# Softmax attention on one Trainium2 core: 64-row products for the maxima, sums in four blocks, the inverse spread by transfers

## The chip, the core and the metric

The kernel runs on one core of a Trainium2 chip. The metric is the device time of one execution in microseconds (us). It computes a small network of six stages on an input of 8 sequences of 512 tokens with 128 features; the change touches one of them, the softmax attention, which is about 40% of the time.

## The reference, cut to what matters

```python
def _L0_attn_ref(x, Wq, Wk, Wv, Wo, bo):          # x: 8 x 512 x 128, 16 heads of 64
    q = split_heads(x @ Wq.T); k = split_heads(x @ Wk.T); v = split_heads(x @ Wv.T)
    sim = jnp.einsum('bhid,bhjd->bhij', q, k) * scale
    attn = safe_softmax(sim)                       # e = exp(s - max); e / (sum(e) + 1e-10)
    out = jnp.einsum('bhij,bhjd->bhid', attn, v)
    return out.transpose(0, 2, 1, 3).reshape(B, N, INNER) @ Wo.T + bo

x = x + 0.5 * _L0_ffn_ref(_layernorm(x, axis=-1), ...)
x = x + _L0_attn_ref(_layernorm(x, axis=-1), ...)  # the stage of this change
x = x + 0.5 * _L0_ffn_ref(...)                     # then a mixture of experts, linear attention,
...                                                # and the experts again
```

## The kernel before, in words

The stages run one after the other; each is a block in which every engine follows its own written-out list, with semaphores between them. The attention stage (`attn_stage`, from L544) works on 64 pairs of heads (8 sequences, 8 pairs each). The loop variable g counts pairs, and one turn of it is called a period here. In period g the engines work on several pairs at once: TensorE projects queries, keys and values of pair g+2, makes the scores of pair g+1 for their maxima, makes the transposed scores of pair g for the exponentials, multiplies pair g-1 with its values, and puts pair g-2 through the output weights. Names, with i as the unit (head i//4, tile of 128 i%4):

- **project** (L840 to L860): three fp16 products of a high and a low part for q and k (512 columns each), twelve of 128 columns for v, all into the one bank `proj`. `high` (L751, ScalarE) writes the fp16 high part from that bank, `low` (L682, VectorE) the low part, `values_in` (L757) the values.
- **to_rows** (L598 to L612, the SyncE queue) copies the parts into operand buffers: `both` holds a head's q with high rows in partitions 0 to 63 and low rows in 64 to 127, and beside it q high once more with a row for the maximum; `kh` holds k high in both halves, `kl` k low and a row of constants. It is 10 transfers a pair.
- **scores** (L806): one fp16 product of 128 rows and 512 columns for each of 8 units, from `both` and `kh`, so q high and q low enter. **neg_max** (L663, VectorE) reduces it to 128 maxima. **max_turned** (L817) transposes the maxima of a head, once per head, `max_row` on VectorE (L671) scales them, and `max_row` on SyncE (L614) copies them into `both`: two small transfers a pair.
- **scores_turned** (L824, products at L836 and L837): two fp16 products of 512 columns per unit, with the maximum already subtracted. **exp** (L765, ScalarE) writes the exponentials `pT`. Two banks take turns, so a unit waits for the exponential two units before.
- GpSimd adds the four tiles of `pT` of each head (L648 to L656). **values** (L862) multiplies this by ones into `sums`, two products of 64 output rows and 512 columns (L868), so that all 128 rows of `sums` hold the sum that belongs to them; then eight products of 64 output rows (L875) into `pv`. `total_out` (L773) copies the sums, `inv_total` (L689) inverts 128x512 on VectorE, `normalise` (L693) multiplies.
- **output** (L879): four fp32 products.

A shared numbering of uses (`bank_use`, `score_use`, `turn_use`) makes the two `score` banks serve the eight scores and the two transposes in order. The order of TensorE in a period stands in its last loop:

```python
for i in range(UPP):                       # 8 units
    if live(g + 1): scores(g + 1, i)
    if live(g):     scores_turned(g, i)
    if i == 1 and live(g):     max_turned(g, 1)
    if i == 2 and live(g + 2): project(g + 2, 0)
    if i == 3: ...                         # output(g-2), project(g+2, 1), max_turned(g+1, 0), values(g-1)
    if i == 6 and live(g + 2): project(g + 2, 2)
```

The functions in full:

Of the kernel before, what the change touches and what calls it, by code (L numbers as in the profile page):

```python
# [10 lines left out]
F16 = mybir.dt.float16  # L11
# [532 lines left out]
def attn_stage(nc, mem, tag):  # L544

    with ExitStack() as ctx:
# [3 lines left out]
        M_UNIT = 64.0  # L552
        both = [s.sb(f"both{i}", [P, 2, 2, SEQ], F16) for i in range(RING)]
        kh = [s.sb(f"kh{i}", [P, 2, SEQ], F16) for i in range(RING)]
        kl = [s.sb(f"kl{i}", [P, 2, SEQ], F16) for i in range(RING)]
        part = [s.sb(f"part_{n}", [P, 2, SEQ], F16) for n in "qk"]
        vv = [s.sb(f"v{i}", [P, TPB, P]) for i in range(4)]
        pT = [s.sb(f"pT{i}", [P, 2, TPB, SEQ]) for i in range(2)]
        psum = [mem["w_attn"][:, i, :].rearrange("p (h q) -> p h q", h=2) for i in range(2)]
        total, rinv = mem["w_attn"][:, 2, 0:SEQ], mem["w_attn"][:, 2, SEQ:2 * SEQ]  # L560
        nmax = [s.sb(f"nmax{i}", [P, P]) for i in range(2)]
        mrow = [s.sb(f"mrow{i}", [TPB, P], F16) for i in range(2)]
        oT = [s.sb(f"oT{i}", [P, SEQ]) for i in range(2)]
        ones = mem["spare"][:, 0:DH]
# [3 lines left out]
        (set_up, proj_done, hi_done, lo_done, v_out, s_done, s_read, t_done, exp_done, chain, added, sums_done, total_done,  # L568
         rinv_done, pv_done, o_done, out_done, biased, x_added) = (s.sem(n) for n in (
             "set_up", "proj_done", "hi_done", "lo_done", "v_out", "s_done", "s_read", "t_done", "exp_done", "chain",  # L570
             "added", "sums_done", "total_done", "rinv_done", "pv_done", "o_done", "out_done", "biased", "x_added"))
        s_in = [s.sem(f"s_in{i}") for i in range(RING)]
        t_in = [s.sem(f"t_in{i}") for i in range(RING)]
        m_in = [s.sem(f"m_in{i}") for i in range(2)]
        S_DMAS, T_DMAS = 8, 2
# [3 lines left out]

        def bank_use(g, j):  # L580

            if g < 0:
                return j if j < 2 else j - 1
            if g == PAIRS_ALL - 1:
                return 9 + 10 * g
            return 9 + 10 * g + j

        UNIT_USE = (0, 1, 3, 4, 6, 7, 8, 9)
        TURN_USE = (5, 2)
        score_use = lambda g, i: bank_use(g - 1, UNIT_USE[i])  # L590
        turn_use = lambda g, head: bank_use(g - 1 + head, TURN_USE[head])

        with nc.Block() as block:

            @block.sync
            def _(sp):
                clear_spent(sp, mem)
                def to_rows(g, which, part_i):  # L598

                    src = part[which]  # L600
                    k = g % RING
                    for head in range(2):
                        rows = src[halves[head], part_i, :]
                        if which == 0 and part_i == 0:
                            sp.dma_start(both[k][0:DH, :, head, :], rows.unsqueeze(1).to_broadcast([DH, 2, SEQ])).then_inc(s_in[k], 16)
                        elif which == 0:
                            sp.dma_start(both[k][DH:P, 0, head, :], rows).then_inc(s_in[k], 16)
                        elif part_i == 0:
                            sp.dma_start(kh[k][0:DH, head, :], rows).then_inc(s_in[k], 16)
                            sp.dma_start(kh[k][DH:P, head, :], rows).then_inc(s_in[k], 16)  # L610
                        else:
                            sp.dma_start(kl[k][0:DH, head, :], rows).then_inc(t_in[k], 16)  # L612

                def max_row(g, head):  # L614

                    sp.wait_ge(s_read, turn_use(g, head) + 1)
                    sp.dma_start(both[g % RING][DH:DH + 1, 1, head, :].rearrange("o (t q) -> o t q", q=P), mrow[head][:])\
                      .then_inc(m_in[head], 16)

                sp.wait_ge(set_up, RING + 3)  # L620
# [42 lines left out]
            def _(dve):  # L663
                def neg_max(g, i):

                    head, qt = divmod(i, TPB)
                    use = score_use(g, i)
                    dve.wait_ge(s_done, use + 1)
                    nc.vector.tensor_reduce(nmax[head][:, qt:qt + 1], score[use % 2][:], AX.X, ALU.max, negate=True)\  # L669
                      .then_inc(s_read, 1)  # L670

                def max_row(g, head):

                    use = turn_use(g, head)
                    dve.wait_ge(s_done, use + 1)
                    if g:
                        dve.wait_ge(m_in[head], 16 * g)
                    nc.vector.tensor_scalar(mrow[head][:], score[use % 2][0:TPB, 0:P], 1.0 / M_UNIT, None, ALU.mult)\
                      .then_inc(s_read, 1)

                def low(g, which):

                    dve.wait_ge(hi_done, 2 * g + 1 + which)
                    scale = (DH ** -0.5 / W_ATTN, 1.0 / W_ATTN)[which]
                    pair = part[which]
                    nc.vector.scalar_tensor_tensor(out=pair[:, 1, :], in0=proj[:], scalar=scale, in1=pair[:, 0, :], op0=ALU.mult,
                                                   op1=ALU.subtract).then_inc(lo_done, 1)
# [12 lines left out]

                def add_x(b):

# [5 lines left out]
                nc.vector.memset(nmax[0][:], 0.0)  # L708
                nc.vector.memset(nmax[1][:], 0.0).then_inc(set_up, 1)
# [4 lines left out]
                dve.wait_ge(set_up, RING + 2)  # L714
# [963 lines left out]
```

## Time and profile before

| | |
|---|---|
| median of 3 runs | 2228.96 us (2228.8 to 2236.12) |
| the profiled execution, its own time | 2225.31 us |
| its span in the trace | 2223.6 us |
| TensorE busy in the span | 1599.6 us, 72% |
| VectorE busy | 1569.2 us, 71% |
| granted TensorE clock, mean | 0.882 |

Busy time is the union of the instructions of an engine. A TensorE record ends later than its columns have streamed, so records overlap, and the distance between two starts is what a product takes of the engine. SPq is the queue from which SyncE issues transfers; such an issue holds only the queue, and its data land later.

### The profile page before, as it was taken

Reading aid. Unit: us, or ns where it says so; the run is one execution under the profiler, and the core shown is the slowest. Engines: PE = TensorE matmul, PEld = TensorE weight load, DVE = VectorE, ACT = ScalarE, POOL = GpSimd, SP = SyncE. Lnnn points to the kernel's source line nnn. Section 1 sums busy time; section 2 is a strip of 40 time slices with the busy share of each in tenths; the row PEclk is TensorE's granted clock in tenths of the full one; section 3 lists DMA queues with packets and bytes.
Section 4 is the critical chain, followed back from the end, with each engine's and each line's share of the span. In section 5 each row is a group of like instructions: output and inputs, shape, how many; then the busy total and the mean of one; then the engine's idle time right before and its main releaser. Section 6 shows DMA issues by size and latency. Waiting matters only on the chain. (4 is left out here: it accounts for less than half of the span.)

```text
span 2223.6 us, 29789 instructions
## 1 busy us (share of the span) xinstructions
PE 1599.6 (72%) x9139; PEld 934.4 (42%) x9139; DVE 1569.2 (71%) x3212; ACT 912.8 (41%) x2102; POOL 1028.3 (46%) x1332
## 2 busy tenths in 40 slices
PE   0546389999999999999965563158658888830686
PEld 0334134444444444444423343135437767730453
DVE  5887778878788888877878886336467777752563
ACT  0112255555555555555522221035336676610452
POOL 0111245555555555555532224635435555546353
PEclk9889599999999999999987895579879999955898
DMA  6000022222222222222200000122300000001224
GB/s 186 0 0 1 23 63 58 58 58 58 63 59 61 60 59 58 58 58 59 62 9 1 0 0 24 56 77 80 104 16 1 1 1 1 1 32 62 75 81 145
DMA packets 126010, 104.05 MB, mean 47 GB/s; under 512 B 19680, under 2 KB 120480, under 8 KB 125856
## 3 DMA queue, kind: packets, MB, share of 16 engines
q1 hardware_dynamic: 111616, 77.75, 13.6%
q0 software_dynamic: 8704, 18.89, 2.5%
q10 hardware_dynamic: 5536, 5.52, 0.8%
q8 instruction: 77, 1.26, 0.2%
q14 instruction: 77, 0.63, 0.1%
HBM read 29.32 MB, written 22.30 MB: 23 GB/s over the span
## 5 line engine op out<-in xcount | busy, mean ns | idle before, releaser
L770 ACT ACTIVATE at_pT<-at_turned 128x512 f32<-128x512 f32 x512 | 305.6, 597 | 290.3 <-PE at_turned L837 271.2
L669 DVE TENSOR_REDUCE at_nmax<-at_score 128x1 f32<-128x512 f32 x512 | 337.1, 680 | 69.8 <-PE at_score L814 66.8
L648 POOL TENSOR_TENSOR m_rows<-at_pT 128x512 f32<-128x512 f32 x128 | 162.5, 1269 | 375.1 <-ACT at_pT L770 375.1
L691 DVE RECIPROCAL m_rows<-m_rows 128x512 f32<-128x512 f32 x64 | 214.6, 3353 | 37.7 <-ACT m_rows L776 37.7
L875 PE MATMUL at_pv<-at_pT,at_v 128*64 128x512 f32 x1024 | 230.6, 592 | 0.0
L814 PE MATMUL at_score<-at_kh,at_both 128*128 128x512 f16 x512 | 196.7, 385 | 22.6 <-DVE at_nmax L669 17.0
L1056 POOL DMA_INDIRECT by_token<-m_ysb,m_dest x144 | 138.2, 960 | 144.7 <-DVE m_ysb L1136 109.5
L836 PE MATMUL at_turned<-at_both,at_kh 128*128 128x512 f16 x512 | 194.9, 381 | 0.4 <-ACT at_pT L770 0.3
L837 PE MATMUL at_turned<-at_both,at_kl 128*128 128x512 f16 x512 | 194.8, 380 | 0.0
L656 POOL TENSOR_TENSOR m_rows<-m_rows,at_pT 128x512 f32<-128x512 f32 x128 | 162.8, 1272 | 10.6 <-ACT at_pT L770 0.7
L652 POOL TENSOR_TENSOR m_rows<-m_rows,at_pT 128x512 f32<-128x512 f32 x128 | 162.7, 1271 | 10.4 <-ACT at_pT L770 0.5
L1050 POOL DMA_INDIRECT by_expert<-m_rows,m_slot x128 | 123.7, 966 | 90.7 <-DVE m_slot L1099 53.0
L419 PE MATMUL f_gate<-m_wguT,f_xqT 128*128 128x352 f32 x128 | 63.1, 581 | 104.2 <-DVEq L337 102.9
L1307 PE MATMUL m_h<-m_w,m_x 128*128 x432 | 113.8, 400 | 33.1 <-DVE m_x L1113 23.2
L875 PEld LDWEIGHTS at_pv<-at_pT,at_v 128*64 128x64 f32 x1024 | 73.6, 137 | 146.2 <-issue 146.2
L365 POOL TENSOR_TENSOR f_hq<-f_hg,f_hsc 128x704 f32<-128x704 f32 x32 | 44.4, 1386 | 194.3 <-DVEq L341 194.3
L854 PE MATMUL at_proj<-m_rows 128*128 128x512 f16 x384 | 107.1, 389 | 18.6 <-DVE at_kl L716 10.3
L115 DVE TENSOR_SCALAR la_xn<-la_y,la_ln_mean,la_ln_rstd 128x128 f32<-128x128 f32 x192 | 81.6, 486 | 52.4 <-POOLq L1478 52.4
L381 ACT ACTIVATE f_silu<-f_gate 128x704 f32<-128x704 f32 x32 | 24.2, 757 | 219.7 <-PE f_up L420 219.7
L814 PEld LDWEIGHTS at_score<-at_kh,at_both 128*128 128x128 f16 x512 | 49.5, 97 | 145.5 <-DVE at_nmax L669 61.7
L1296 PE MATMUL m_x<-m_ident,m_xin 128*128 128x128 f32 x144 | 23.0, 284 | 88.6 <-DMA m_xin<-by_expert 88.6
L1124 DVE SCALAR_TENSOR_TENSOR m_g<-m_h,m_xin,m_silu 128x256 f32<-128x256 f32 x144 | 65.3, 478 | 28.1 <-ACT m_silu L1220 14.3
(309 smaller groups left out, 3685.0 us busy)
## 6 DMA issues: line engine op xcount, KB each, us to landing
at_both<-at_part_q SPq DMA_DIRECT2D x128, 128.0 KB, 2.4
at_kh<-at_part_k SPq DMA_DIRECT2D x256, 64.0 KB, 2.0
m_xin<-by_expert SPq DMA_DIRECT2D x144, 72.0 KB
at_both<-at_part_q SPq DMA_DIRECT2D x128, 64.0 KB, 2.1
at_kl<-at_part_k SPq DMA_DIRECT2D x128, 64.0 KB
m_rows<-by_token SPq DMA_DIRECT2D x32, 256.0 KB, 4.8
by_token<-m_ysb,m_dest POOLq DMA_INDIRECT x144
m_x<-in_x SPq DMA_DIRECT2D x8, 256.0 KB, 4.7
```

What stands on the lines that cost most here:

```text
L648: nc.gpsimd.tensor_tensor(acc, pT[g % 2][:, head, 0, :], pT[g % 2][:, head, 1, :], ALU.add).then_inc(chain, 1)
L652: nc.gpsimd.tensor_tensor(acc, acc, pT[g % 2][:, head, 2, :], ALU.add).then_inc(chain, 1)
L656: nc.gpsimd.tensor_tensor(acc, acc, pT[g % 2][:, head, 3, :], ALU.add).then_inc(added, 1)
L669: nc.vector.tensor_reduce(nmax[head][:, qt:qt + 1], score[use % 2][:], AX.X, ALU.max, negate=True)\
L691: nc.vector.reciprocal(rinv, total).then_inc(rinv_done, 1)
L770: nc.scalar.activation(pT[g % 2][:, head, kt, :], turned[i % 2][:], ACT.Exp).then_inc(exp_done, 1)
L814: nc.tensor.matmul(score[use % 2][:], both[k][:, 0, head, qt * P:(qt + 1) * P], kh[k][:, head, :], start=True, stop=True).then_inc(s_done, 1)
L836: nc.tensor.matmul(turned[i % 2][:], kh[k][:, head, tile], both[k][:, 0, head, :], start=True, stop=False)
L837: nc.tensor.matmul(turned[i % 2][:], kl[k][:, head, tile], both[k][:, 1, head, :], start=False, stop=True)\
L875: last = nc.tensor.matmul(pv[halves[head], :], vv[g % 4][:, kt, halves[head]], pT[g % 2][:, head, kt, :], start=(kt == 0), stop=(kt == TPB ...
L1050: nc.gpsimd.indirect_dma_start(dram_rows, bass.IndirectOffsetOnAxis(slot[:, k, t:t + 1], 0), rows[k][:, t, :], None).then_inc(scattered, 16)
L1056: nc.gpsimd.indirect_dma_start(mem["dram_y_all"], bass.IndirectOffsetOnAxis(dest[j // TPB % DESTS][:, j % TPB:j % TPB + 1], 0), ysb[q % YS ...
```

## The change

Six parts, all in `attn_stage`.

1. The scores for the maxima use the high parts alone, straight from the projected tiles in SBUF: 64 rows per head, the two heads in rows 0 to 63 and 64 to 127, one after the other in program order, into the two `score` banks. The high parts get two buffers each. The scores no longer wait for transfers.
2. One transpose of a 128x8 tile of maxima per pair, into a corner of the `sums` bank, one scaling and one transfer in place of two of each. It now comes behind the k rows of the next pair on SyncE.
3. The sums are four products of 32 output rows and 256 columns, each (head, half of the queries) in a block of 32 partitions. `total_out` and the reciprocal work on 128x256.
4. One row of each block is spread to the 64 partitions of its head by four transfers (`spread`), and `normalise` waits for these and runs one period later.
5. The values of pair g are projected in period g, at its end; `v` has two buffers, and `oT` one.
6. The order of every engine's list changes. SyncE in period g: q rows and k rows of g+2, `max_row(g+1)`, `spread(g-1)`. TensorE: eight units, the products with the values at the end of the period, with the transpose and the projection of v in between.

`high` now waits also for the scores of pair g-2 of its buffer, and `values_in(g)` for `values(g-2)`; the small helpers keep their forms (the diff is cut, its indentation shortened).

```diff
+def q_rows(g):
     k = g % RING
+    sp.wait_ge(hi_done, 2 * g + 1)
     for head in range(2):
+        sp.dma_start(both[k][0:DH, :, head, :],
+                     head_of[0][g % 2][halves[head], :].unsqueeze(1).to_broadcast([DH, 2, SEQ])).then_inc(q_in[k], 16)
+    sp.wait_ge(lo_done, 2 * g + 1)
+    for head in range(2):
+        sp.dma_start(both[k][DH:P, 0, head, :], rest_of[0][halves[head], :]).then_inc(q_in[k], 16)
+def k_rows(g):
+    k = g % RING
+    sp.wait_ge(hi_done, 2 * g + 2)
+    for head in range(2):
+        for half in halves:
+            sp.dma_start(kh[k][half, head, :], head_of[1][g % 2][halves[head], :]).then_inc(k_in[k], 16)
+    sp.wait_ge(lo_done, 2 * g + 2)
+    for head in range(2):
+        sp.dma_start(kl[k][0:DH, head, :], rest_of[1][halves[head], :]).then_inc(k_in[k], 16)
+def max_row(g):
+    sp.wait_ge(m_out, g + 1)
+    sp.dma_start(both[g % RING][DH:DH + 1, 1, :, :].rearrange("o h (t q) -> o (h t) q", q=P), mrow[:]).then_inc(m_in, 16)
+def spread(g):
+    sp.wait_ge(packed_done, g + 1)
+    if g:
+        sp.wait_ge(o_done, g)
+    for head in range(2):
+        for half in range(2):
+            first = (2 * head + half) * QUAD
+            sp.dma_start(rinv[halves[head], half * HALF:(half + 1) * HALF],
+                         packed[first:first + 1, :].unsqueeze(1).to_broadcast([1, DH, HALF])).then_inc(rinv_in, 16)
...
+sp.wait_ge(set_up, RING + 2)
 for g in PERIODS:
-    if live(g):
-        max_row(g, 1)
     if live(g + 2):
         if g + 2 >= RING:
             sp.wait_ge(t_done, 8 * (g + 3 - RING))
-        sp.wait_ge(hi_done, 2 * (g + 2) + 1)
-        to_rows(g + 2, 0, 0)
-        sp.wait_ge(lo_done, 2 * (g + 2) + 1)
-        to_rows(g + 2, 0, 1)
+        q_rows(g + 2)
+        k_rows(g + 2)
     if live(g + 1):
-        max_row(g + 1, 0)
-    if live(g + 2):
-        sp.wait_ge(hi_done, 2 * (g + 2) + 2)
-        to_rows(g + 2, 1, 0)
-        sp.wait_ge(lo_done, 2 * (g + 2) + 2)
-        to_rows(g + 2, 1, 1)
+        max_row(g + 1)
+    if live(g - 1):
+        spread(g - 1)
...
+def neg_max(g, qt):
+    if qt == 0 and g:
+        dve.wait_ge(m_done, g)
+    for head in range(2):
+        dve.wait_ge(s_done, 8 * g + 2 * qt + head + 1)
+        nc.vector.tensor_reduce(nmax[:, head * TPB + qt:head * TPB + qt + 1], score[head][:], AX.X, ALU.max, negate=True)\
+          .then_inc(s_read, 1)
...
-def inv_total(g):
+def invert(g):
     dve.wait_ge(total_done, g + 1)
-    nc.vector.reciprocal(rinv, total).then_inc(rinv_done, 1)
+    if g:
+        dve.wait_ge(rinv_in, 16 * R_DMAS * g)
+    nc.vector.reciprocal(packed, total).then_inc(packed_done, 1)
 def normalise(g):
     dve.wait_ge(pv_done, g + 1)
-    dve.wait_ge(rinv_done, g + 1)
-    if g >= 2:
-        dve.wait_ge(out_done, g - 1)
-    nc.vector.tensor_tensor(oT[g % 2][:], pv[:], rinv, ALU.mult).then_inc(o_done, 1)
+    dve.wait_ge(rinv_in, 16 * R_DMAS * (g + 1))
+    if g:
+        dve.wait_ge(out_done, g)
+    nc.vector.tensor_tensor(oT[:], pv[:], rinv, ALU.mult).then_inc(o_done, 1)
...
 for g in PERIODS:
     if live(g + 1):
         neg_max(g + 1, 0)
+    if live(g - 2):
+        normalise(g - 2)
+    if live(g + 1):
         neg_max(g + 1, 1)
-    if live(g):
-        max_row(g, 1)
+    if live(g + 2):
+        low(g + 2, 0)
     if live(g + 1):
         neg_max(g + 1, 2)
         neg_max(g + 1, 3)
     if live(g + 2):
-        low(g + 2, 0)
+        low(g + 2, 1)
     if live(g + 1):
-        max_row(g + 1, 0)
-    if live(g + 2):
-        low(g + 2, 1)
+        max_row(g + 1)
     if live(g - 1):
-        inv_total(g - 1)
-    if live(g + 1):
-        neg_max(g + 1, 4)
-        neg_max(g + 1, 5)
-    if live(g - 1):
-        normalise(g - 1)
-    if live(g + 1):
-        neg_max(g + 1, 6)
-        neg_max(g + 1, 7)
+        invert(g - 1)
...
 for g in PERIODS:
     if live(g):
         exp(g, 0)
         exp(g, 1)
-        exp(g, 2)
     if live(g + 2):
         high(g + 2, 0)
     if live(g):
-        exp(g, 3)
+        for i in range(2, 6):
+            exp(g, i)
     if live(g + 2):
         high(g + 2, 1)
+    if live(g):
+        exp(g, 6)
+        exp(g, 7)
     if live(g - 1):
         total_out(g - 1)
     if live(g):
-        for i in range(4, 7):
-            exp(g, i)
-    if live(g + 2):
-        values_in(g + 2)
-    if live(g):
-        exp(g, 7)
+        values_in(g)
...
+def scores(g, qt):
+    if qt == 0:
+        pe.wait_ge(hi_done, 2 * g + 2)
+    if g or qt:
+        pe.wait_ge(s_read, 8 * g + 2 * qt)
+    for head in range(2):
+        rows = halves[head]
+        nc.tensor.matmul(score[head][:], head_of[0][g % 2][rows, qt * P:(qt + 1) * P], head_of[1][g % 2][rows, :],
+                         start=True, stop=True).then_inc(s_done, 1)
+
+def max_turned(g):
+    pe.wait_ge(s_read, 8 * (g + 1))
+    if g:
+        pe.wait_ge(m_out, g)
+    if g >= 2:
+        pe.wait_ge(total_done, g - 1)
+    nc.tensor.transpose(max_bank, nmax[:], mem["ident"][:]).then_inc(m_done, 1)
...
-        pe.wait_ge(t_in[k], 16 * T_DMAS * (g // RING + 1))
-    if kt == 0:
-        pe.wait_ge(m_in[head], 16 * (g + 1))
+        pe.wait_ge(q_in[k], 16 * Q_DMAS * (g // RING + 1))
+        pe.wait_ge(k_in[k], 16 * K_DMAS * (g // RING + 1))
+        pe.wait_ge(m_in, 16 * (g + 1))
...
+    if which == 0:
+        if g >= 3:
+            pe.wait_ge(v_out, g - 2)
+        if g:
+            pe.wait_ge(lo_done, 2 * g)
     elif which == 1:
         pe.wait_ge(lo_done, 2 * g + 1)
-    elif which == 2:
-        pe.wait_ge(lo_done, 2 * g + 2)
+    else:
+        pe.wait_ge(lo_done, 2 * min(g + 3, PAIRS_ALL))
+        if g:
+            pe.wait_ge(v_out, g)
...
+def add_up(g):
     pe.wait_ge(added, 2 * (g + 1))
     if g:
         pe.wait_ge(total_done, g)
+    pe.wait_ge(m_out, min(g + 2, PAIRS_ALL))
     for head in range(2):
+        for half in range(2):
+            first = (2 * head + half) * QUAD
+            last = nc.tensor.matmul(sums[first:first + QUAD, 0:HALF], ones[:],
+                                    psum[g % 2][:, head, half * HALF:(half + 1) * HALF], start=True, stop=True)
     last.then_inc(sums_done, 1)
...
 for g in PERIODS:
     for i in range(UPP):
-        if live(g + 1):
-            scores(g + 1, i)
         if live(g):
             scores_turned(g, i)
-        if i == 1 and live(g):
-            max_turned(g, 1)
-        if i == 2 and live(g + 2):
+        if i % 2 == 0 and live(g + 1):
+            scores(g + 1, i // 2)
+        if i == 1 and live(g + 2):
             project(g + 2, 0)
-        if i == 3:
-            if live(g - 2):
-                output(g - 2)
-            if live(g + 2):
-                project(g + 2, 1)
-            if live(g + 1):
-                max_turned(g + 1, 0)
-            if live(g - 1):
-                values(g - 1)
-        if i == 6 and live(g + 2):
-            project(g + 2, 2)
+        if i == 3 and live(g - 2):
+            output(g - 2)
+        if i == 5 and live(g + 2):
+            project(g + 2, 1)
+    if live(g - 1):
+        add_up(g - 1)
+        values(g - 1, 0)
+    if live(g + 1):
+        max_turned(g + 1)
+    if live(g - 1):
+        values(g - 1, 1)
+    if live(g):
+        project(g, 2)
+    if live(g - 1):
+        values(g - 1, 2)
+        values(g - 1, 3)
```

## Rows read from the trace of the kernel before

**Rows 1.** The page: busy time by engine, and two lines of its 40 slices.

```profile
PE 1599.6 (72%) x9139; PEld 934.4 (42%) x9139; DVE 1569.2 (71%) x3212; ACT 912.8 (41%) x2102; POOL 1028.3 (46%) x1332
...
PE   0546389999999999999965563158658888830686
...
PEclk9889599999999999999987895579879999955898
```

**Rows 2.** Busy by window: start and end, length, engines, clock, DMA share, GB/s.

```profile
601.13:614.59 13.46, 13.15 (x74) 5.87 (x73) 10.81 (x15) 7.17 (x12) 7.58 (x6) 1.00 0.22 55
```

**Rows 3.** Timeline (start, length, engine, line, operation): reciprocals of consecutive periods.

```profile
611.90 3.35 DVE L691 RECIPROCAL m_rows<-m_rows 128x512 f32<-128x512 f32 x1 [0.44 <-ACT m_rows L776]
...
625.36 3.35 DVE L691 RECIPROCAL m_rows<-m_rows 128x512 f32<-128x512 f32 x1 [0.44 <-ACT m_rows L776]
...
639.31 3.35 DVE L691 RECIPROCAL m_rows<-m_rows 128x512 f32<-128x512 f32 x1 [0.44 <-ACT m_rows L776]
```

**Rows 4.** Timeline of one period, the lines on which durations and handovers rest.

```profile
608.17 1.05 PE L887 MATMUL at_out<-m_woT,at_oT 128*128 128x128 f32 x8
...
609.28 0.82 PE L854 MATMUL at_proj<-m_rows 128*128 128x512 f16 x3
...
609.94 0.27 PE L822 MATMUL at_score<-m_ident,at_nmax 128*128 128x128 f32 x1
...
610.14 1.08 PE L868 MATMUL at_sums<-m_rows 128*64 128x512 f32 x4
...
611.05 3.60 PE L875 MATMUL at_pv<-at_pT,at_v 128*64 128x512 f32 x16
...
614.59 0.39 PE L814 MATMUL at_score<-at_kh,at_both 128*128 128x512 f16 x1
...
614.82 0.38 PE L836 MATMUL at_turned<-at_both,at_kh 128*128 128x512 f16 x1
...
615.03 0.38 PE L837 MATMUL at_turned<-at_both,at_kl 128*128 128x512 f16 x1
...
615.17 1.22 DVE L669 TENSOR_REDUCE at_nmax<-at_score 128x1 f32<-128x512 f32 x2
...
615.45 1.89 ACT L770 ACTIVATE at_pT<-at_turned 128x512 f32<-128x512 f32 x3 [3.58 <-PE at_turned L837]
...
616.54 0.83 PE L858 MATMUL at_proj<-m_rows 128*128 128x128 f16 x12
```

**Rows 5.** Instruction groups from 500 to 900 us (busy, mean ns, idle before).

```profile
L669 DVE TENSOR_REDUCE at_nmax<-at_score 128x1 f32<-128x512 f32 x235 | 154.7, 680 | 28.1 <-PE at_score L814 26.7
...
L691 DVE RECIPROCAL m_rows<-m_rows 128x512 f32<-128x512 f32 x30 | 100.6, 3353 | 13.1 <-ACT m_rows L776 13.1
...
L814 PE MATMUL at_score<-at_kh,at_both 128*128 128x512 f16 x235 | 89.7, 382 | 7.0 <-DVE at_nmax L669 7.0
...
L686 DVE SCALAR_TENSOR_TENSOR at_part_k<-at_proj,at_part_k 128x512 f16<-128x512 f32 x30 | 20.8, 692 | 7.2 <-ACT at_part_k L755 7.2
...
L678 DVE TENSOR_SCALAR at_mrow<-at_score 4x128 f16<-4x128 f32 x59 | 16.2, 274 | 30.8 <-PE at_score L822 30.8
```

**Rows 6.** Timeline of the SyncE queue: the maxima's transfer, then the k rows.

```profile
624.48 0.66 SPq L617 DMA_DIRECT2D at_both<-at_mrow  x1
625.18 0.48 SPq L609 DMA_DIRECT2D at_kh<-at_part_k  x1
...
627.62 1.24 SPq L612 DMA_DIRECT2D at_kl<-at_part_k  x2
```

**Rows 7.** The page's DMA issues (size, median us to landing), and landings at L607.

```profile
at_both<-at_part_q SPq DMA_DIRECT2D x128, 128.0 KB, 2.4
at_kh<-at_part_k SPq DMA_DIRECT2D x256, 64.0 KB, 2.0
...
DMA to landing us min/median/max: 2.0/2.1/3.3
```

More of the change, by code:

```diff
@@ L555, in attn_stage @@
         kl = [s.sb(f"kl{i}", [P, 2, SEQ], F16) for i in range(RING)]
-        part = [s.sb(f"part_{n}", [P, 2, SEQ], F16) for n in "qk"]
-        vv = [s.sb(f"v{i}", [P, TPB, P]) for i in range(4)]
+        head_of = [[s.sb(f"high_{n}{i}", [P, SEQ], F16) for i in range(2)] for n in "qk"]
+        rest_of = [s.sb(f"low_{n}", [P, SEQ], F16) for n in "qk"]
+        vv = [s.sb(f"v{i}", [P, TPB, P]) for i in range(2)]
         pT = [s.sb(f"pT{i}", [P, 2, TPB, SEQ]) for i in range(2)]
         psum = [mem["w_attn"][:, i, :].rearrange("p (h q) -> p h q", h=2) for i in range(2)]
[L560 to L564, printed above, removed]
+        total, packed, rinv = mem["w_attn"][:, 2, 0:HALF], mem["w_attn"][:, 2, HALF:SEQ], mem["w_attn"][:, 2, SEQ:2 * SEQ]
+        nmax = s.sb("nmax", [P, UPP])
+        mrow = s.sb("mrow", [UPP, P], F16)
+        oT = s.sb("oT", [P, SEQ])
+        ones = mem["spare"][:, 0:QUAD]
         score = [s.bank(f"score{i}") for i in range(2)]
@@ L567, in attn_stage @@
         pv, sums, proj, out = (s.bank(n) for n in ("pv", "sums", "proj", "out"))
[L568 to L575, printed above, removed]
+        max_bank = sums[0:UPP, HALF:HALF + P]
+        (set_up, qk_done, v_done, hi_done, lo_done, v_out, s_done, s_read, m_done, m_out, m_in, t_done, exp_done, chain, added,
+         sums_done, total_done, packed_done, rinv_in, pv_done, o_done, out_done, biased, x_added) = (s.sem(n) for n in (
+             "set_up", "qk_done", "v_done", "hi_done", "lo_done", "v_out", "s_done", "s_read", "m_done", "m_out", "m_in", "t_done",
+             "exp_done", "chain", "added", "sums_done", "total_done", "packed_done", "rinv_in", "pv_done", "o_done", "out_done",
+             "biased", "x_added"))
+        q_in = [s.sem(f"q_in{i}") for i in range(RING)]
+        k_in = [s.sem(f"k_in{i}") for i in range(RING)]
+        Q_DMAS, K_DMAS, R_DMAS = 4, 6, 4
         halves = (slice(0, DH), slice(DH, P))
@@ L597, in _ @@
                 clear_spent(sp, mem)
-                def to_rows(g, which, part_i):
-                    src = part[which]
+                def q_rows(g):
                     k = g % RING
+                    sp.wait_ge(hi_done, 2 * g + 1)
                     for head in range(2):
[L603 to L612, printed above, removed]
@@ L801, in _ @@
                 XY = [(0, 0), (0, 1), (1, 0)]
[L803 to L822 removed]
+                def scores(g, qt):
[11 more added lines that the diff above has]
+                        pe.wait_ge(m_out, g)
+                    if g >= 2:
+                        pe.wait_ge(total_done, g - 1)
+                    nc.tensor.transpose(max_bank, nmax[:], mem["ident"][:]).then_inc(m_done, 1)
                 def scores_turned(g, i):
@@ L859, in project @@
                                                         start=(i == 0), stop=(i == 2))
-                    last.then_inc(proj_done, 1)
-                def values(g):
+                        last.then_inc(v_done, 1)
+                def add_up(g):
                     pe.wait_ge(added, 2 * (g + 1))
@@ L866, in values @@
                         pe.wait_ge(total_done, g)
+                    pe.wait_ge(m_out, min(g + 2, PAIRS_ALL))
                     for head in range(2):
-                        last = nc.tensor.matmul(sums[halves[head], :], ones[:], psum[g % 2][:, head, :], start=True, stop=True)
+                        for half in range(2):
+                            first = (2 * head + half) * QUAD
+                            last = nc.tensor.matmul(sums[first:first + QUAD, 0:HALF], ones[:],
+                                                    psum[g % 2][:, head, half * HALF:(half + 1) * HALF], start=True, stop=True)
                     last.then_inc(sums_done, 1)
-                    pe.wait_ge(v_out, g + 1)
-                    if g:
-                        pe.wait_ge(o_done, g)
-                    for kt in range(TPB):
-                        for head in range(2):
-                            last = nc.tensor.matmul(pv[halves[head], :], vv[g % 4][:, kt, halves[head]], pT[g % 2][:, head, kt, :],
-                                                    start=(kt == 0), stop=(kt == TPB - 1))
-                    last.then_inc(pv_done, 1)
+                def values(g, kt):
+                    if kt == 0:
+                        pe.wait_ge(v_out, g + 1)
+                        if g:
+                            pe.wait_ge(o_done, g)
+                    for head in range(2):
+                        last = nc.tensor.matmul(pv[halves[head], :], vv[g % 2][:, kt, halves[head]], pT[g % 2][:, head, kt, :],
+                                                start=(kt == 0), stop=(kt == TPB - 1))
+                    if kt == TPB - 1:
+                        last.then_inc(pv_done, 1)
                 def output(g):
```

87 lines of the change are left out of this document (23 added, 64 removed).

## The prediction

> **What bounds the kernel now.** I began with the page's lines over 40 slices [rows 1]: in slices 6 to 19 TensorE is at nine tenths or more at full granted clock, so there the attention stage is TensorE's. The busy time of one period [rows 2] says the same: 13.15 of 13.46 us for TensorE, 10.81 VectorE, 7.17 ScalarE, 7.58 GpSimd. The starts of the reciprocal [rows 3] give the period: 13.46 us, and 13.95 where a sequence ends (8 of 64), 13.52 on average. I treat the stage as 64 periods, so 0.1 us a period is 6.4 us of the whole.
>
> Busy is not work, so I took stream times from distances between starts [rows 4]. A 512-column fp16 product takes 0.215 us (614.82 to 615.03) though its record lasts 0.38; the tail is 0.165. Two 64-row-output products of 512 fp32 columns run side by side: four such pairs, 3.60 less the tail, are 3.44 us, 0.86 a pair. Sums: 611.05 - 610.14 = 0.91, a pair and 0.05. One group less its tail: output 0.885, three projection products 0.65, twelve small ones 0.665. Transpose 0.10 to 0.11.
>
> A change of the shape of the array's tiles costs something: the last pair of values streams until 611.05 + 3.44 = 614.49, and the first transposed product starts at 614.82; less 0.215 for the score between them, 0.115 is left. Into the sums it is 610.14 less (609.94 + 0.11) = 0.09. I take 0.115.
>
> One period before, by this: 8 scores 1.72, 16 transposed 3.44, q and k 1.30, v 0.665, output 0.885, sums 0.91, values 3.44, two transposes 0.22, two changes 0.23: 12.81. So 0.65 of the 13.46 is waiting, mostly for the reductions (7.0 us in 29.4 pairs at the scores on TensorE's own rows [rows 5], the rest before weight loads).
>
> **The change, part by part.**
>
> *Scores.* Two products of 64 rows use different halves of the array. No row shows such a pair. Bounds: side by side, as the column halves are [rows 4], 0.215 plus 0.05 for the second load; one after the other 0.43 and perhaps a visible weight load. I take 0.265, since the nearest row is the pair of column halves: four pairs are 1.06 against 1.72, 0.66 saved. But they stand alone between full-array products: eight new changes of shape, 0.92. So the part **loses 0.26 us** of TensorE time. The page of the Trainium skill "TensorEngine Tiling (Array Packing)", Key Properties, says that tiles work independently but that a change of mode drains the array; the trace agrees with the second (0.09 and 0.115) and shows the first for columns only. If its drain were the full tail of 0.165, the sum below would be the case of dear changes.
>
> *Sums.* Four blocks of 256 columns: 0.43 + 0.05 if all four run together, 0.91 if two by two. The column pair is the nearest row; I take 0.48, saving 0.43. One more shape (32 after 64): one more change, 0.115.
>
> *Transpose.* One less: 0.11 saved. It and the v projection stand inside the values: two changes each, 0.46.
>
> *TensorE's sum:* 3.44 + 1.06 + 1.30 + 0.885 + 0.48 + 3.44 + 0.11 + 0.665 = 11.38, and 15 changes (8 scores, 2 at the sums, 4 inside, 1 back) x 0.115 = 1.73: 13.11 us. It is more than 12.81. A gain can thus only come from the 0.65 us of waiting.
>
> *Do the waits go?* I wrote the new period out from its first transposed product at 0, with handovers as in [rows 4]: start of the last product to ScalarE or VectorE 0.42 (615.03 to 615.45), exponentials 0.63 apart, reductions 0.6 apart, record 0.68. Scores 0 at 0.55, reduced by 2.24. Unit 1, q projected until 2.00, unit 2 until 2.43, scores 1 at 2.55 (needs 2.24). The inverse may let `normalise` start at 2.4, ended 3.08; then the reductions to 4.28, q low 4.88, output 3.36 to 4.24. Scores 2 at 4.78 (needs 4.28), k projected 5.59 to 6.24 (needs q low), scores 3 at 6.78 (needs 6.48), unit 7 until 7.59. ScalarE, with eight exponentials and two `high` in this stretch, stays ahead: exponential 5 ends at 6.40, unit 7 starts at 7.16. Sums 7.71 to 8.19, values 0 to 9.16, transpose 9.28 (reductions end 8.48, `total_out` 9.03), values 1 to 10.36, v 10.48 to 11.14 (k low 9.08), values 2 and 3 to 12.97, next period at 13.09. Nothing waits, with 0.25 to 0.5 us to spare. The margin comes from two scores at a time, and from the reciprocal: 3353 ns [rows 5] becomes some 1.68 on half the columns, so VectorE has 9.4 us of work where it had 10.8 (eight reductions at 0.68 and two lows at 0.69, `normalise` like them, 0.27 and 1.68 [rows 5], less the overlap of records).
>
> *SyncE.* Each issue holds its queue 0.53 to 0.7 us [rows 6]: 12 a pair become 15, about 9.4 us of 13. `high` of k ends at 7.04, four k transfers from 7.11 to 9.56, two more to 10.84, and only then the maxima's transfer, which all of the next period waits for. Its landing is not shown. Bounds: 128 KB land in 2.4 us, 64 KB in 2.0 [rows 7], so at nearly no data 1.6; upper end 2.4. At 1.8 it lands at 12.64, at 2.4 at 13.29. I take 1.8: hidden by 0.4. The `spread` issues follow at 11.55 (after the reciprocal, 9.86 to 11.54) and the last at 13.45; landing 2.0 as the k rows puts the inverse at 15.45, that is 2.4 in the next period. The added 256 KB a period is a third more than 768 KB, against a DMA share of 0.22 [rows 2]: no limit in bandwidth.
>
> *Costed at nothing:* `values_in` now follows `total_out`; the cover is the values 2 and 3, and without it project q of the next period would start later by as much. Halving `v` and `oT`: their readers are over 2 us earlier than their writers in the list above. `high`'s wait for scores of pair g-2: a whole period old. GpSimd's adds are unchanged and end some 4 us before the sums. The additions at sequence ends (0.5 us each now) fall in a stretch in which VectorE is idle. Start of the stage: the scores no longer wait for k rows, some 2 to 3 us less; end: the inverse takes four issues and a landing, 1.9 + 2.0, less 1.7 of reciprocal, 2 us more. Together zero.
>
> *Sum:* 13.09 against 13.52 is 0.43 a period, 64 x 0.43 = 27.5 us. The profiled execution of 2225.31 becomes 2197.8; the median of 2228.96 lies 3.7 above it, so 2201.5 by that. I say **2200 us**, 1.3% faster. Its own range, changes from 0.09 to 0.125 and the maxima's landing up to 2.4: period 12.75 to 13.3, 2180 to 2215.
>
> **Rivals.**
>
> *Cheaper changes (2165).* If weights for one half load while the full array still streams, changes around the scores cost next to nothing. TensorE's sum is 12.2, and the SyncE chain sets the end: 7.11 comes down by some 0.5, 12.64 becomes 12.1 to 12.5 with landings of 1.8 to 2.2. 12.5 means 64 x 1.02 = 65 us less. For it: full-array loads do overlap [rows 4]; against it: both changes measured cost 0.09 or more. "TensorE: Matmul & The Clock Gate" of the Trainium skill, Part 3, states that loads to other row groups overlap running products; no row here shows it.
>
> *Row halves do not run together, or changes are dear (2250, slower).* Place: the four score pairs. Serial products add 0.165 each, a visible load 0.1: 4 x 0.265 = 1.06; the period is 14.0 to 14.15, 64 x 0.5 = 32 us more at the worst, 13 with the load hidden. A change at the full tail (0.165) adds 15 x 0.05 = 0.75 and gives the same. It decides from 0.43 us of TensorE time more than I count.
>
> *The inverse lands late (2250, slower).* Place: `normalise` stands on VectorE between the first and second reductions, and scores 1, the output and all behind wait. There is no slack from a landing of about 2.3 us on, and each us more costs one: 3.3 us, plausible for 64 rows read from one partition, gives 14.0. Against it: 64 KB rows land in 2.0, 2.1 at L607 though up to 3.3 [rows 7].
>
> *No change (2229).* The four blocks of sums run two by two (+0.43): 13.52, exactly the old period; the change would then not do what it says. Waits at long issues or landings in SyncE's chain could do it too.
>
> **How the numbers follow.** Forecast 0.50; cheaper changes 0.14; halves not together or dear changes 0.16; late inverse 0.08; no change 0.12. A measurement tells about 0.5%, 11 us, from no change. Faster: 0.45 of the forecast, since its edge with 13.3 reaches near the bound, and 0.14: 0.59. Slower: 0.24, less 0.02 for serial pairs with loads hidden that stay within 11 us: 0.22. Within: 0.19. The range of 8 in 10 takes the forecast, most of the fast case and the slow ones up to about 2250: 2165 to 2250.
>
> **What would show it.** Period from the reciprocals near 13.1. The starts of two score products a few tens of ns apart (if 0.2 us apart, they are serial), and score to next transposed product. Sums from start to first value 0.5. VectorE busy about 9.5 us a period. The first transposed product of a period starting right behind the values, or, in the SyncE case, behind the landing of the maxima's row; `normalise` waiting for a transfer until about 2.4 us. The forecast is wrong if TensorE idles over 0.5 us a period at a transfer, or if score pairs cost over 0.6 us with their changes.

## The result, and the profile after

The changed kernel takes 2737.25 us (2734.89 to 2738.49), the kernel before, measured beside it, 2231.31 us: ratio 1.226, 95% interval 1.224 to 1.229, so 506 us slower where 29 us faster was forecast. The page of the kernel after, its busy line and slices, to be read against [rows 1]:

```profile
PE 1730.8 (63%) x9331; PEld 932.4 (34%) x9331; DVE 1446.6 (53%) x3146; ACT 886.3 (32%) x2102; POOL 1029.1 (38%) x1332
...
PE   1563677667777667777677763653186588873386
...
PEclk9895888888888878888888885885598799995698
...
DMA  5000344443334433344433330000223000001224
```

The DMA line of the kernel before:

```profile
DMA  6000022222222222222200000122300000001224
```

TensorE is no longer full in the attention stage, and its granted clock is below full there. Its busy time rose from 1599.6 to 1730.8 us, at a mean clock of 0.815 where it was 0.882; VectorE and ScalarE work less than before, GpSimd as much. What rose by more than its work is the DMA engines' busy share: 3 to 4 tenths instead of 2, although the bytes of the stage only rose by a third. The timeline of one period of the kernel after:

```profile
600.90 0.64 PE L855 MATMUL at_sums<-m_rows 128*32 128x256 f32 x8
...
601.47 1.08 PE L865 MATMUL at_pv<-at_pT,at_v 128*64 128x512 f32 x4
...
603.00 1.73 DVE L688 RECIPROCAL m_rows<-m_rows 128x256 f32<-128x256 f32 x1
...
604.04 0.70 SPq L615 DMA_DIRECT2D at_both<-at_mrow  x1
...
604.85 3.48 SPq L624 DMA_DIRECT2D m_rows<-m_rows  x4
...
606.34 0.39 PE L816 MATMUL at_turned<-at_both,at_kh 128*128 128x512 f16 x1
...
606.57 0.38 PE L817 MATMUL at_turned<-at_both,at_kl 128*128 128x512 f16 x1
...
606.88 0.39 PE L794 MATMUL at_score<-at_high_k,at_high_q 64*128 64x512 f16 x2
...
607.20 0.39 PE L816 MATMUL at_turned<-at_both,at_kh 128*128 128x512 f16 x1
...
615.14 0.69 DVE L695 TENSOR_TENSOR at_oT<-at_pv,m_rows 128x512 f32<-128x512 f32 x1 [6.49 <-issue]
...
615.89 2.08 PE L877 MATMUL at_out<-m_woT,at_oT 128*128 128x128 f32 x8 [6.14 <-DVE at_oT L695]
```

The period starts at 606.34. The four spread transfers (L624) are issued from 604.85, and `normalise` (L695) starts at 615.14, after 6.5 us in which VectorE had nothing it was allowed to do. TensorE waits 6.1 us for it at the output, and the output then takes 2.08 us where it took 1.05 [rows 4]. For this wait the profile names no releaser ("issue"). Of the things that `normalise` waits for only the spread is this late; the landings at L624, the windows around it, and the DMA issues from 600 to 1000 us say so (in a window line the last three numbers are granted clock, DMA share and GB/s):

```profile
DMA to landing us min/median/max: 4.5/6.0/8.4
```
```profile
607.00:608.00 1.00, 1.00 (x6) 0.41 (x5) 0.63 (x2) 0.74 (x2) 0.00 (x0) 1.00 0.90 30
...
613.00:614.00 1.00, 0.00 (x0) 0.00 (x0) 0.00 (x0) 0.00 (x0) 0.00 (x0) 0.50 0.69 136
...
615.10:620.00 4.90, 4.11 (x16) 2.48 (x17) 3.23 (x6) 0.80 (x2) 0.00 (x0) 0.61 0.11 28
```
```profile
at_kh<-at_high_k SPq DMA_DIRECT2D x76, 64.0 KB, 2.0
m_rows<-m_rows SPq DMA_DIRECT2D x76, 64.0 KB, 6.0
```

While the spread runs (first window) the DMA engines are 90% busy and move 30 GB/s. The k rows, which move as many bytes between as many rows, still land in 2.0 us. TensorE stands idle from 609.9 us on; its granted clock is at half (1.2 GHz) in the second window, and still 0.61 on average in the third, after work has come back.

### The profile page after: what moved, and what is told of

It reads as the page before. It is cut to its first block and busy times, and to the rows that moved or that the text cites. A ratio compares the mean times of both kernels' runs of the same rounds, so it can differ in the third digit from the quotient of the medians.

```text
span 2736.8 us, 30613 instructions
## 1 busy us (share of the span) xinstructions
PE 1730.8 (63%) x9331; PEld 932.4 (34%) x9331; DVE 1446.6 (53%) x3146; ACT 886.3 (32%) x2102; POOL 1029.1 (38%) x1332
## 3 DMA queue, kind: packets, MB, share of 16 engines
q8 instruction: 79, 1.29, 0.2%
## 5 line engine op out<-in xcount | busy, mean ns | idle before, releaser
L877 PE MATMUL at_out<-m_woT,at_oT 128*128 128x128 f32 x512 | 132.8, 441 | 398.9 <-DVE at_oT L695 398.9
L695 DVE TENSOR_TENSOR at_oT<-at_pv,m_rows 128x512 f32<-128x512 f32 x64 | 44.3, 692 | 425.0 <-issue 399.1
L865 PE MATMUL at_pv<-at_pT,at_v 128*64 128x512 f32 x1024 | 261.6, 611 | 0.0
L877 PEld LDWEIGHTS at_out<-m_woT,at_oT 128*128 128x128 f32 x512 | 114.0, 328 | 431.3 <-DVE at_oT L695 431.3
L816 PE MATMUL at_turned<-at_both,at_kh 128*128 128x512 f16 x512 | 225.4, 440 | 16.9 <-DMA at_both<-at_mrow 16.3
L817 PE MATMUL at_turned<-at_both,at_kl 128*128 128x512 f16 x512 | 219.9, 429 | 0.0
L838 PE MATMUL at_proj<-m_rows 128*128 128x512 f16 x384 | 120.0, 427 | 12.9 <-DVE at_kl L709 9.6
L688 DVE RECIPROCAL m_rows<-m_rows 128x256 f32<-128x256 f32 x64 | 110.7, 1730 | 9.9 <-ACT m_rows L762 9.9
L794 PE MATMUL at_score<-at_high_k,at_high_q 64*128 64x512 f16 x512 | 112.5, 436 | 3.5 <-DVE at_nmax L669 2.7
L816 PEld LDWEIGHTS at_turned<-at_both,at_kh 128*128 128x128 f16 x512 | 54.3, 106 | 158.5 <-issue 135.7
```

The lines of the kernel that those rows point to most:

```text
L816: nc.tensor.matmul(turned[i % 2][:], kh[k][:, head, tile], both[k][:, 0, head, :], start=True, stop=False)
L817: nc.tensor.matmul(turned[i % 2][:], kl[k][:, head, tile], both[k][:, 1, head, :], start=False, stop=True)\
L865: last = nc.tensor.matmul(pv[halves[head], :], vv[g % 2][:, kt, halves[head]], pT[g % 2][:, head, kt, :], start=(kt == 0), stop=(kt == TPB ...
L877: last = nc.tensor.matmul(out[:, tile], oT[:, tile], mem["woT"][:, pair, :], start=(pair == 0 and t == 0), stop=(pair == PAIRS - 1), skip_ ...
```

## The experiments

Theory S: a spread transfer reads one row 64 times and is served slowly at its source. Rivals: Q, four more transfers on the SyncE queue are late whatever they read; B, a repeated source is slow as such. Periods below are the mean distance of the reciprocals between 560 and 1000 us (last start less first, over 20 to 33 distances; the kernel before has 13.52). e2, e3 and e5 leave the right inverse out for some or all queries, so they do not compute the reference. The diffs are cut to the lines that matter. The last four kernels ran on a chip on which everything is faster (before: 2148.13 us), so ratios are to be compared.

| run | source rows of a spread | us | before | ratio | period |
|---|---|---|---|---|---|
| after | 1 | 2737.25 | 2231.31 | 1.226 (1.224 to 1.229) | 21.49 |
| e1_from32 | 32 | 2242.25 | 2233.51 | 1.0039 (1.0028 to 1.005) | 13.57 |
| e2_from64 | 64 | 2230.41 | 2233.51 | 0.999, one run | 13.39 |
| e3_no_spread | none | 2205.41 | 2233.51 | 0.9875 (0.9858 to 0.9891) | 13.00 |
| e4_full_sums | none | 2215.36 | 2233.51 | 0.9911 (0.9892 to 0.993) | 13.20 |
| e5_half_bytes | 1, half the bytes | 2313.34 | 2225.57 | 1.039, one run | 14.95 |
| e6_from8 | first 8 | 2482.50 | 2225.57 | 1.115, one run | 17.33 |
| e7_row1_late | 1 | 2463.44 | 2225.57 | 1.1062 (1.1038 to 1.1087) | 17.02 |
| e8_full_wide | none | 2208.74 | 2225.57 | 0.9915 (0.9897 to 0.9934) | 13.21 |
| e9_from8_apart | every fourth of 32 | 2159.28 | 2148.13 | 1.005, one run | 13.47 |
| e10_from16 | first 16 | 2173.46 | 2148.13 | 1.012, one run | 13.73 |
| e11_from32_mid | 32 | 2151.32 | 2148.13 | 1.0017 (1.0007 to 1.0026) | 13.50 |
| e12_wide_order | none | 2120.61 | 2148.13 | 0.9872 (0.9856 to 0.9889) | 13.01 |

**Other source rows.** All 32 rows of a block of `sums` are equal, so more of them can be read with the same result:

```diff
-    packed[first:first + 1, :].unsqueeze(1).to_broadcast([1, DH, HALF])
+    packed[first:first + QUAD, :].unsqueeze(1).to_broadcast([QUAD, 2, HALF])      # e1
+    packed[halves[head], :]                                                        # e2
```

> The changed kernel with one edit: each of the four spread transfers reads the 32 equal rows of its block twice each, instead of one row 64 times. Same bytes, same number of issues, same queue, same waits, same result. Theory S (64 reads of one partition are served one after the other; 256 KB in about 9 us): landing falls from 6 us to about 2, normalise no longer waits, the period falls from 21.5 to about 12.8 us (TensorE stream times as the trace after shows them), total about 2185 us. Theory Q (four more issues and transfers on the SyncE queue are what is late, whatever they read): landing stays at 5 to 6 us, total stays near 2737 us. Theory B (a broadcast source, read more than once, is slow as such): still over 4 us to landing, total 2500 or more.

> As the run before, but each spread transfer reads 64 different rows of the same tile, so no row twice; half of the rows then carry the inverse of the other half of the queries. Theory S: same as reading 32 rows, landing 2.0 us, total about 2185. Theory B: only here landing comes down to 2 us, and this run is much faster than the one with 32 rows. Theory Q: no change from 2737 us.

S holds: one slice of one line takes away 22 of the 22.6%. Q is out, and B as well, since 32 rows read twice land in 2.1 us, near the 2.0 of unrepeated rows. DMA issues of e1, and its `normalise`:

```profile
m_rows<-m_rows SPq DMA_DIRECT2D x120, 64.0 KB, 2.1
```
```profile
609.36 0.69 DVE L695 TENSOR_TENSOR at_oT<-at_pv,m_rows 128x512 f32<-128x512 f32 x1 [0.97 <-issue]
```

I expected 2185; it is 2242. The period was to be 12.8 and is 13.57. `normalise` still waits in e1, 16.3 us in 29 periods from 600 to 1000 us, and TensorE for it at the output, 6.3 us in 16 of them; in 9 periods TensorE also waits for the maxima's row, 4.3 us together.

**No spread at all.** The transfers and the waits for them go, `rinv` is set to one once.

```diff
-    sp.dma_start(rinv[halves[head], half * HALF:(half + 1) * HALF], packed[first:first + 1, :]...)
-    dve.wait_ge(rinv_in, 16 * R_DMAS * (g + 1))
+    nc.vector.memset(rinv, 1.0)
```

> The spread transfers are left out and normalise multiplies with a constant tile, set once; the reciprocal still runs. Theory S or B: about what 32 rows give, or 0 to 30 us less since the SyncE queue issues 11 instead of 15 a period: 2160 to 2185 us. If this is still over 2300, another wait than the one for the inverse holds the period. Theory Q agrees with S here.

**Parts 3 and 4 undone**, sums and reciprocal on 128x512, no transfer.

```diff
-    last = nc.tensor.matmul(sums[first:first + QUAD, 0:HALF], ones[:],
-                            psum[g % 2][:, head, half * HALF:(half + 1) * HALF], start=True, stop=True)
+    last = nc.tensor.matmul(sums[halves[head], :], ones[:], psum[g % 2][:, head, :], start=True, stop=True)
-    nc.vector.reciprocal(packed, total).then_inc(packed_done, 1)
+    nc.vector.reciprocal(rinv, total).then_inc(packed_done, 1)
```

> Parts 3 and 4 of the change undone alone: sums in two blocks of 64 rows and 512 columns, the reciprocal on 128x512 straight into the tile that normalise reads, no spread; scores of 64 rows, single transpose and the new order stay. TensorE 0.45 us more per period than with four blocks, VectorE 1.6 us more (about 11 of 13). Theory S: period 13.1 to 13.3, total 2200 to 2215 us, so the other parts by themselves are a small gain over the kernel before. Rival (the 64-row scores and the order cost what they save): 2225 to 2240 us.

e4 came out at the slow edge of its range (2215.36), e3 20 us above its own: I had put it at 2185 at most. Both are far from 2300, so no other wait of the new order is large. One is left in e3: TensorE waits for the maxima's row in 8 of 31 periods, 2.9 us together, and only the periods without such a wait take 12.89 us. The other parts are a gain of 0.9%, and the four blocks with their shorter reciprocal are worth about 0.4% more (10 us by the medians), while the transfers that they need cost 1.6% (e1 against e3) even when they read 32 rows.

**Bytes or reads.** Columns `0:P` of each half alone are spread; half of the queries keep an inverse of one. And 8 rows, read 8 times:

```diff
-    packed[first:first + 1, :].unsqueeze(1).to_broadcast([1, DH, HALF])
+    packed[first:first + 1, 0:P].unsqueeze(1).to_broadcast([1, DH, P])             # e5
+    packed[first:first + 8, :].unsqueeze(1).to_broadcast([8, 8, HALF])             # e6
```

> The changed kernel, but each spread transfer carries 128 of its 256 columns, so 64 reads of 512 bytes from the one partition; the other columns of the inverse stay at one, so half of the queries are not normalised. If the one partition gives bytes at a fixed rate (about 30 GB/s, as the trace after shows while the spread runs), the four transfers take half as long, the last lands some 4 us sooner, the period falls from 21.5 to about 17 us and the total to 2440 to 2500. If each read costs the same whatever its size (34 ns), nothing changes: 2737.

> Each spread transfer reads 8 equal rows 8 times each. If what counts is how often one partition is read, the cost falls eightfold and landing is 2 to 3 us, total 2235 to 2260. If it falls with the number of source rows only slowly (or if few source rows also mean few engines), landing is 3 to 5 us and the total 2300 to 2500.

Bytes it is: landing fell from 6.0 to 3.4 us.

```profile
DMA to landing us min/median/max: 3.0/3.4/3.9
```

The total fell further than expected (2313 where I had 2440 to 2500). From the first issue to `normalise` it is now 5.43 us (600.30 to 605.73) instead of 10.29, 0.9 more than the 4 us I had expected to save, and with the shorter idling the clock stays up: mean clock 0.88 against 0.815, and the output takes 1.16 us instead of 2.08. But e6 missed S as I had put it. Eight rows are eight times fewer reads per row, and the loss was only halved. Two windows in e6 in which its spread runs:

```profile
617.00:618.00 1.00, 1.00 (x6) 0.31 (x5) 0.22 (x1) 0.60 (x1) 0.00 (x0) 1.00 0.44 49
618.00:619.00 1.00, 1.00 (x6) 0.39 (x4) 1.00 (x2) 0.70 (x2) 0.01 (x1) 1.00 0.45 49
```

49 GB/s from eight rows against 30 from one. So the limit is not the single row alone, and two readings are left. Eight source rows may keep only half of the DMA engines at work, since their share is 0.44 where it was 0.90; or neighbouring rows share something. The Trainium skill has a rule of the second kind, in "SBUF — State Buffer", Door 1: groups of four neighbouring partitions share one of 16 ports for transfers, 32 neighbours reach 8 of them. The test for it keeps the number of rows, and moves them apart:

```diff
-    packed[first:first + 8, :].unsqueeze(1).to_broadcast([8, 8, HALF])
+    packed[first:first + QUAD:4, :].unsqueeze(1).to_broadcast([8, 8, HALF])
```

> As the run with 8 equal rows read 8 times each, but the rows are every fourth of the block's 32 instead of the first 8. Same number of source rows, of reads per row, of bytes and issues. The Trainium skill, SBUF - State Buffer, Door 1, says that four neighbouring partitions share one of 16 ports; by it the first 8 rows lie behind 2 ports and these behind 8, as all 32 do. Theory P (the port of the source is the limit, about 27 to 30 GB/s each): as with 32 rows, landing near 2 us, total 2235 to 2260. Theory R (reads of one partition follow each other, or only 8 of 16 engines work when there are 8 source rows): no change from 2482.

> Each spread transfer reads the first 16 rows of its block 4 times. Theory P: 4 ports, four times the rate of one row, 64 KB in about 0.6 us, as fast as the queue issues them; landing about 2.2 us, total 2240 to 2290. Theory R with engines: all 16 engines work, so 2240 as well; it differs from P in the run before only.

Theory P holds: 1.005 against 1.115 with the same eight reads of eight rows, so neither the reads per row nor the number of source rows is the limit, but which rows they are. Each is one run, but they are 11 points apart. That the group is four rows was not tested by itself. Sixteen neighbours land in 2.4 us (1.012). `normalise` in e9, beside its spread:

```profile
602.62 2.62 SPq L624 DMA_DIRECT2D m_rows<-m_rows  x4
...
606.86 0.69 DVE L695 TENSOR_TENSOR at_oT<-at_pv,m_rows 128x512 f32<-128x512 f32 x1 [0.43 <-issue]
```

From first issue to `normalise` it is 4.24 us; in the kernel after it was 10.29.

**Place.** In e7 `normalise(g - 2)` moves behind `neg_max(g + 1, 3)` and the output with it; e11, with 32 rows, has it behind `neg_max(g + 1, 1)` and at `i == 5`.

```diff
-                        if i == 3 and live(g - 2):
+                        if i == 7 and live(g - 2):
```

> The changed kernel with the same spread from one row; only the place is moved: normalise behind the last reduction of the period instead of behind the first, the output behind unit 7 instead of unit 3. Theory S with place: the landing is still 10 us after the first issue, but about 5 us more of TensorE's work lies before it; the loop from the spread to the next first product with values gives 14.2 to 15.5 us a period, total 2280 to 2360. Rival (the transfers also hold up the queue and everything on it, so that the place does not matter): 2650 or more.

> 32 source rows, and normalise one step later on VectorE (behind the second pair of reductions, the output behind unit 5). If what is left against the run without a spread (2205) is the wait of normalise for landings of 2.1 to 2.9 us, this ends it: 2205 to 2220. If it is the longer SyncE list that delays the maxima's row, nothing is gained: 2240.

The place is worth about a tenth of the time: the same slow transfers cost 1.106 instead of 1.226, but e7 came out at 17.0 us a period, not 14.2 to 15.5. Its timeline:

```profile
609.08 0.69 DVE L695 TENSOR_TENSOR at_oT<-at_pv,m_rows 128x512 f32<-128x512 f32 x1 [0.77 <-issue]
...
609.82 1.62 PE L877 MATMUL at_out<-m_woT,at_oT 128*128 128x128 f32 x8 [2.30 <-DVE at_oT L695]
...
614.58 1.73 DVE L688 RECIPROCAL m_rows<-m_rows 128x256 f32<-128x256 f32 x1
...
616.34 3.52 SPq L624 DMA_DIRECT2D m_rows<-m_rows  x4
```

I had left out that the output, the next sums and the reciprocal stand between `normalise` and the next spread: 7.26 us (609.08 to 616.34), and 10.25 from there to the next `normalise` at 626.59, make 17.5, the length of most periods. e11 missed too: `normalise` no longer waits, which was to bring nearly all of the distance to e3, but the third scores now wait 0.35 us in every period for the reductions that it delays (below). So 1.0017 is all it gives, against 1.0039.

```profile
606.75 0.39 PE L794 MATMUL at_score<-at_high_k,at_high_q 64*128 64x512 f16 x2 [0.35 <-DVE at_nmax L669]
```

**Part 1 undone too**, on top of e4: the products have 128 rows again, the two heads in turn. And then, in e12, the transpose put behind `values(g - 1, 1)`.

```diff
-    nc.tensor.matmul(score[head][:], head_of[0][g % 2][rows, qt * P:(qt + 1) * P], head_of[1][g % 2][rows, :],
+    nc.tensor.matmul(score[head][:], both[k][:, 0, head, qt * P:(qt + 1) * P], kh[k][:, head, :],
```

> The run with sums in two blocks and no spread, and part 1 undone as well: the maxima's scores are again 128-row products from the operand buffers, two heads one after the other. TensorE: 8 x 0.215 = 1.72 a period against 4 x 0.415 = 1.66 with the changes of shape around the 64-row pairs. Theory: part 1 is worth almost nothing, within 10 us of 2215 either way. Rival (the 64-row pair is the gain): 45 us slower, 2260.

> The run with full sums and 128-row scores, and one more edit: the transpose of the maxima moves behind the second pair of values, next to the projection of v, so that two changes of shape inside the values go (0.2 us a period, 13 us in all), while the SyncE queue still has k rows to issue when the maxima are ready. Expected 2195 to 2205, ratio about 0.986. If the maxima's row then lands too late, 2210 or more.

e8 and e4 are the same, 0.9915 and 0.9911: the 64-row pairs gain nothing, and the 0.9% comes from the parts that both keep (2, 5 and 6). e12 is the fastest kernel that computes the reference, 1.3% below before. Its transpose and projection now start 0.11 us apart, where in the kernel after there were 1.2 us and two more changes between (602.48 and 603.70):

```profile
606.77 0.27 PE L798 MATMUL at_sums<-m_ident,at_nmax 128*8 128x128 f32 x1
606.88 0.83 PE L838 MATMUL at_proj<-m_rows 128*128 128x128 f16 x12
```

## Why the prediction was wrong

**The step that failed** is the `spread` in the SyncE part: "landing 2.0 as the k rows puts the inverse at 15.45, that is 2.4 in the next period". The k rows have the same size and the same number of packets, and differ in what decided: they read 64 partitions. The median landing was 6.0 us, and since a transfer (64 KB at 30 GB/s, 2.2 us) takes longer than an issue (0.6 us), the four pile up (landings from 4.5 to 8.4 us): 10.29 us from the first issue to `normalise`, where I had 1.9 + 2.0 = 3.9. The inverse arrived at 8.80 in the period (615.14 - 606.34), not at 2.4.

**The rival was named, with its place right and its price wrong.** "The inverse lands late" had `normalise` between the first and second reductions, landings hidden up to 2.3 us, each us more costing one, and 0.08 of chance; I stopped at 3.3 us, the longest landing of an unlike transfer [rows 7]. The bound was no bound: no row showed many reads of one partition, though the rival itself spoke of "64 rows read from one partition". Two smaller sums of the rivals are off as well. Serial products with the load hidden give 13.75 us a period, 15 us more in all and not 13; a change at the full tail gives 13.84, 20 us more, and not "the same" as 14.0 to 14.15.

**A second term was missing**: idle TensorE costs clock. Against e3, `normalise` starts 6.57 us later in the period (8.80 against 610.68 - 608.45 = 2.23), and the rest of the period is 1.27 longer (11.93 against 10.66), which is where the clock stands at 0.5 and 0.61; the output alone has 1.03 of it. That is 7.84 of 20.73 us; over all periods it is 21.49 - 13.00 = 8.49, times 64 is 543 us, and the measured distance from e3 is 532.

**A third, which the slow reads cover up:** the SyncE chain has less to spare than the forecast gave it. With landings of 2.1 us, nearly the 2.0 that I had, e1 is still 0.4% slower than the kernel before. In its shortest periods `normalise` starts 2.66 us after the first transposed product (662.76 - 660.10), where I had 2.4, and they last 13.17 us, 0.28 more than e3's. The longer ones, up to 14.32 us, are those in which the inverse comes later still, or the maxima's row does. The row is late when issues before it in the queue are slow, as in the longest kind of period of the kernel after:

```profile
644.07 2.18 SPq L611 DMA_DIRECT2D at_kl<-at_low_k  x2
...
646.30 0.70 SPq L615 DMA_DIRECT2D at_both<-at_mrow  x1
...
648.31 0.38 PE L816 MATMUL at_turned<-at_both,at_kh 128*128 128x512 f16 x1 [0.59 <-DMA at_both<-at_mrow]
```

Two issues of k's low rows take 2.18 us instead of 1.23, the row is issued 1.99 us after the start of the reciprocal instead of 1.04, and TensorE waits for it. The forecast had the row hidden by 0.4 us, with even issues.

**What held.** Without the spread a period without a late row is 12.89 us in e3, forecast 13.09, and the time 28 us under before, forecast 27.5. That the two times agree so well is partly luck: e3 has none of the spread that the forecast kept, and its mean period of 13.00 would give 33 us by the forecast's own rule. TensorE was a little cheaper than priced: a pair of scores with both its changes takes 607.20 - (606.57 + 0.215) = 0.415 us, I had 0.115 + 0.265 + 0.115 = 0.495. The two products together have a record of 0.39 us, a single one 0.38, so the array's row halves do work side by side, and a change costs about 0.1 each way. That a change of mode drains the array is what the Trainium skill's page "TensorEngine Tiling (Array Packing)", Key Properties, says; the trace agrees that it costs time. By these prices part 1 saves 0.06 us a period (1.66 against 1.72), and e8 against e4 shows no difference. I had it lose 0.26. The sums took 0.57 with their change (600.90 to 601.47), forecast 0.595: four blocks run together. The maxima's row was in time in 13 of 19 periods of the kernel after; in the others TensorE waited up to 0.9 us. The gain is in the waiting, as the sum said: of 0.65 us a period nothing is left in the 12.89 us periods of e3, where TensorE has a little more to do than before.

## What to carry to other kernels

Price a transfer by the rows that it reads, and not by its size alone: one row that was spread to 64 partitions was read at 30 GB/s here, and four such transfers in a row added up to 10.3 us. Where equal rows exist, read more of them, and not neighbours: eight rows, four apart, did nearly as well as 32. Have the place of the consumer in mind too, which was worth a tenth of the time. A single pair of products that uses half of the array gains nothing between full ones, since each change of shape cost 0.1 us here, half of a 512-column product; that many such pairs in a row would gain is to be expected, and was not run.

## What was not expected of the hardware

Reads from one partition went at 30 GB/s with 16 DMA engines 90% busy, reads from 8 neighbours at 49 GB/s, and from 8 rows four apart the spread was over in 4.2 us. The Trainium skill's page "SBUF — State Buffer", Door 1, gives 435 GB/s for all 16 ports; by that, an estimate of mine, one port gives 435/16 = 27 GB/s and two give 54. Eight neighbours stayed below their 54. One row gave 23 to 31 GB/s in the windows between 606.5 and 610 us, mostly above its 27; where the two differ, the measured rate counts.

While the slow reads were under way, issues on the same queue took longer as well: the two of the q rows 3.53 us (from 609.16) in the kernel after, 1.29 us (from 608.89) in e1.

Two issues of k's low rows take 1.23 us in most periods, but 1.8 to 2.4 in some, in e1, e3 and e11 too. The single long periods come from there: in e11 the longest, 14.47 us among ones of 13.37, follows such an issue of 2.44 us, and TensorE waits 1.04 us for the maxima's row in it. e12 never waits for the row between 560 and 1000 us. Why single issues take longer stays open.
